# A gated delta-rule block on one core: the two lowest of four inverse-merge levels on narrow tiles, and the state evictions moved to ScalarE

## The reference, cut to what matters

```python
def step(S, inp):
    qt, kt, vt, gt, bt = inp
    S = S * jnp.exp(gt)[..., None, None]
    mem = jnp.einsum('bhk,bhkv->bhv', kt, S)
    delta = (vt - mem) * bt[..., None]
    S = S + jnp.einsum('bhk,bhv->bhkv', kt, delta)
    o = jnp.einsum('bhk,bhkv->bhv', qt * scale, S)
    return (S, o)
```

## Time and profile before

| | |
|---|---|
| median of 3 runs | 2520.83 us (2520.28 to 2522.46) |
| the profiled execution's own time | 2518.24 us |
| its span, first to last instruction | 2516.3 us |
| mean granted TensorE clock | 0.978 |
| PE busy | 2352.5 us, 93% |
| DVE busy | 2004.9 us, 80% |
| ACT busy | 1407.4 us, 56% |
| POOL busy | 1279.2 us, 51% |

### The profile page before, as it was taken

One profiled execution on the slowest core, in us unless ns is written; L12 is line 12 of the kernel. 1 busy time (PEld: TensorE's weight loads), 2 busy tenths in 40 slices (PEclk: granted clock), 3 DMA queues, 4 the chain that ended last, 5 costly groups with the idle time before them and its releaser, 6 DMA issues. The chain is left out here.

```text
span 2516.3 us, 53535 instructions
## 1 busy us (share of the span) xinstructions
PE 2352.5 (93%) x18800; PEld 1889.7 (75%) x18800; DVE 2004.9 (80%) x4146; ACT 1407.4 (56%) x3331; POOL 1279.2 (51%) x2046
## 2 busy tenths in 40 slices
PE   6599999999999999999999999999999998699997
PEld 2378888888888888888888888888888887546665
DVE  5678888888888888888888888888888887235544
ACT  3256666666666666666666666666666665322221
POOL 3456566666666666666666666656566665100000
PEclk9689999999999999999999999999999999799998
DMA  4211121112111211121112111211121110221100
GB/s 129 69 36 35 27 61 34 34 33 55 35 36 36 54 37 35 36 54 36 36 36 55 36 36 36 55 36 36 36 55 36 36 26 9 66 62 34 34 9 9
DMA packets 203849, 103.20 MB, mean 41 GB/s; under 512 B 97009, under 2 KB 185018, under 8 KB 203586
## 3 DMA queue, kind: packets, MB, share of 16 engines
q1 hardware_dynamic: 203266, 99.65, 17.0%
q10 hardware_dynamic: 320, 0.13, 0.0%
HBM read 69.89 MB, written 2.54 MB: 29 GB/s over the span
## 5 line engine op out<-in xcount | busy, mean ns | idle before, releaser
L861 DVE SCALAR_TENSOR_TENSOR dr_y<-dr_ps,cw,dr_y 128x255 f32<-128x255 f32 (+2 forms) x1152 | 479.9, 472 | 8.9 <-ACT dr_y L986 8.9
L1125 POOL TENSOR_TENSOR dr_fo<-dr_vo,dr_nhalf 128x4 f32<-128x4 f32 x128 | 156.1, 1219 | 539.5 <-DVE dr_vo L941 539.5
L744 PE MATMUL dr_ps<-dr_w,dr_am 128*128 128x96 f32 x3072 | 418.1, 280 | 3.2 <-ACT dr_w L1038 3.2
L744 PEld LDWEIGHTS dr_ps<-dr_w,dr_am 128*128 128x128 f32 x3072 | 380.3, 193 | 12.1 <-ACT dr_w L1038 3.9
L831 DVE TENSOR_TENSOR dr_w<-dr_ps,mask 128x512 bf16<-128x512 f32 x512 | 350.3, 684 | 31.4 <-PE dr_ps L629 24.6
L986 ACT ACTIVATE dr_y<-dr_ps,cw 128x256 f32<-128x256 f32 x384 | 160.9, 470 | 195.1 <-PE dr_ps L676 195.0
L1038 ACT COPY dr_w<-dr_ps 128x384 f32<-128x384 f32 x384 | 188.8, 492 | 134.8 <-PE dr_ps L744 134.8
L972 ACT CAST dr_tn<-dr_ps 128x512 bf16<-128x512 f32 x384 | 226.3, 589 | 55.7 <-PE dr_ps L644 55.6
L873 DVE TENSOR_TENSOR_SCAN dr_dec<-dr_abc,dr_dg 128x512 f32<-128x512 f32 x128 | 208.4, 1628 | 33.4 <-POOL dr_dg L1091 18.1
L975 ACT CAST dr_tt<-dr_ps 128x512 bf16<-128x512 f32 x384 | 233.5, 608 | 0.0
L650 PE MATMUL dr_ps<-dr_tt,dr_w 128*128 128x128 bf16 x2048 | 197.9, 219 | 20.1 <-DVE dr_w L831 20.1
(11 more groups left out here) (204 smaller groups left out, 5059.9 us busy)
## 6 DMA issues: line engine op xcount, KB each, us to landing
dr_abc<-scr_a SPq DMA_DIRECT2D x64, 512.0 KB, 5.4
dr_qk<-dr_sy SPq DMA_DIRECT2D x384, 48.0 KB, 2.0
dr_bcb<-scr_b SPq DMA_DIRECT2D x128, 64.0 KB, 4.6
dr_c<-dr_b SPq DMA_DIRECT2D x512, 4.0 KB, 1.8
dr_qk<-dr_sy SPq DMA_DIRECT2D x128, 32.0 KB, 1.9
ex_modb<-scr_mod SPq DMA_DIRECT2D x4, 1024.0 KB, 8.1
wv<-in_Wv SPq DMA_DIRECT2D x8, 384.0 KB, 3.5
wo<-in_Wo SPq DMA_DIRECT2D x1, 3072.0 KB, 12.1
```

The source lines that it names most:

```text
L744: last = pe.matmul(ps[:, bank, h * DV:(h + 1) * DV], wt(h), x[:, h * DV:(h + 1) * DV], start=(start and h == 0), stop=(h == QH - 1), skip_ ...
L861: v.scalar_tensor_tensor(y[:, slot, x:T], ps[:, BANK[n], off:off + T - x], cw[:, t, TAPS - 1 - x:TAPS - x], y[:, slot, x:T], ALU.mult, ALU ...
```

## The change

The two lowest levels (8 to 16, 16 to 32) no longer work on 128x128 tiles. What is not zero there fits in 32 columns per unit. A new POOL piece `block` makes `b32`, the part of `b16` inside the 32x32 diagonal blocks. `narrow1` is a matmul of `b32` with `c32t` (32 columns, all 8 units in one bank) and one masking eviction to `w32` by DVE; `narrow2` is one matmul with `tt`, evicted by ACT to `c32t`; `widen` (DVE) transposes `c32t` to `c32` and expands it to the new `tt`, and after the second narrow level `tn` too. The two upper levels stay as they were. The eviction of `S` moves from DVE to ACT, in front of the squares of the same piece. `PLAN` is another table.

```diff
-LEVELS = 4
-LVL0 = 3
+NARROW = 2
+LEVELS = 2
+LVL0 = 5
...
             def merge1(st, l, g):
                 it, m = st
                 if l == 0:
-                    pe.wait_ge(s["te_ok"], it * 2 + 1)
-                    if g == 0:
-                        pe.wait_ge(s["ab_ok"], it + 1)
-                        wait(pe, s["tt_ok"], (it * LEVELS - 1) * 2 + 1 if it else 0)
+                    pe.wait_ge(s["te_ok"], it * (NARROW + 2) + NARROW + 1)
...
+            def narrow1(st, l):
+                it, m = st
+                if l == 0:
+                    pe.wait_ge(s["ab_ok"], it + 1)
+                    pe.wait_ge(s["b32_ok"], (it + 1) * CH)
+                    pe.wait_ge(s["c32t_ok"], it * (NARROW + 1) + 1)
+                else:
+                    pe.wait_ge(s["cn_ok"], it * NARROW + l)
+                for u in range(U):
+                    last = pe.matmul(ps[:, X0, u * 4 * BASE:(u + 1) * 4 * BASE], b32[:, u, :], c32t[:, u, :],
+                                     start=True, stop=True)
+                last.then_inc(s["n1_ps"], 1)
+
+            def narrow2(st, l):
+                it, m = st
+                pe.wait_ge(s["wn_ok"], it * NARROW + l + 1)
+                pe.wait_ge(s["te_ok"], it * (NARROW + 2) + l + 1)
+                if l == 0:
+                    wait(pe, s["tt_ok"], it * LEVELS * 2)
+                for u in range(U):
+                    last = pe.matmul(ps[:, X1, u * 4 * BASE:(u + 1) * 4 * BASE], tt[:, u, :], w32[:, u, :],
+                                     start=True, stop=True)
+                last.then_inc(s["n2_ps"], 1)
...
             def expand(st):
                 it, m = st
                 v.wait_ge(s["xb_ok"], it + 1)
+                wait(v, s["te_ok"], it * (NARROW + 2))
...
                 v.wait_ge(s["c32_ok"], it + 1)
-                v.transpose(c32t[:].rearrange("p u i -> p (u i)"), c32[:].rearrange("p u i -> p (u i)")
-                            ).then_inc(s["c32t_ok"], 1)
+                turned(c32t, c32).then_inc(s["c32t_ok"], 1)
                 wait(v, s["p3"], it * LEVELS * 2)
...
+                spread(tt, c32).then_inc(s["te_ok"], 1)
+
+            def narrow1(st, l):
+                it, m = st
+                v.wait_ge(s["n1_ps"], it * NARROW + l + 1)
+                wait(v, s["n2_ps"], it * NARROW + l)
+                v.tensor_tensor(w32[:], ps[:, X0, 0:NCOL].rearrange("p (u n) -> p u n", u=U), bc(maskn[:, l, :], 1, U),
+                                ALU.mult).then_inc(s["wn_ok"], 1)
+
+            def widen(st, l):
+                it, m = st
+                v.wait_ge(s["cn_ok"], it * NARROW + l + 1)
+                v.wait_ge(s["te_ok"], it * (NARROW + 2) + l + 1)
+                if l == NARROW - 1:
+                    spread(tn, c32t).then_inc(s["te_ok"], 1)
+                turned(c32, c32t).then_inc(s["c32t_ok"], 1)
+                v.wait_ge(s["c32t_ok"], it * (NARROW + 1) + l + 2)
+                spread(tt, c32).then_inc(s["te_ok"], 1)
...
+            def narrow2(st, l):
+                it, m = st
+                act.wait_ge(s["n2_ps"], it * NARROW + l + 1)
+                act.wait_ge(s["c32t_ok"], it * (NARROW + 1) + l + 1)
+                act.copy(c32t[:], ps[:, X1, 0:NCOL].rearrange("p (u n) -> p u n", u=U)).then_inc(s["cn_ok"], 1)
...
+            def state(st):
+                it, m = st
+                act.wait_ge(s["s_ps"], it + 1)
+                for side in range(2):
+                    lo = 64 * side
+                    act.copy(S[lo:lo + 64, :, side * DV:(side + 1) * DV],
+                             ps[lo:lo + 64, CX, 0:QV].rearrange("p (a n) -> p a n", a=PAIRS)[:, :, side * DV:(side + 1) * DV]
+                             ).then_inc(s["S_ok"], 1)
+                squares(st, 0)
...
+            def block(st):
+                it, m = st
+                wait(pool, s["n1_ps"], it * NARROW)
+                for c in range(CH):
+                    us = slice(c * QH, (c + 1) * QH)
+                    pool.wait_ge(s["b16_ok"], it * CH + c + 1)
+                    pool.tensor_tensor(b32[:, us, :], b16[:, m, us, :], bc(bd32[:], 1, QH), ALU.mult).then_inc(s["b32_ok"], 1)
```

`spread(dst, src)` is the multiply with `bd32` that `expand` held, and `turned(dst, src)` the transpose. Of the new table two lines:

```diff
+        (23.53, ("block",)), (24.9, ("rows",)), (25.89, ("base",)), (29.53, ("expand",)), (30.44, ("narrow1", 0)),
+        (30.64, ("narrow2", 0)), (30.75, ("widen", 0)), (31.96, ("narrow1", 1)), (33.43, ("narrow2", 1)),
```

More of the change, by code:

```diff
@@ L61 @@
 ATANH = [1.0 / (2 * k + 1) for k in range(9)]
[L63 to L70, removed]
[5 rows of a table removed]
[L76 to L80, removed]
@@ L539, in slots @@
                     on[piece[0]](stages[k], *piece[1:])
+        NCOL = U * 4 * BASE
+        wide = lambda ap: ap.rearrange("p u (n i) -> p u n i", i=4 * BASE)
         def run(eng, on):
@@ L547, in delta_rule @@
         PIECES = ("merge1", "merge2", "w0", "delta", "residual", "ks", "out", "state_out", "mean", "gated", "oT", "wo",
-                  "acc", "rows", "base", "expand", "proj", "silu", "taps", "gate", "norms", "gains", "root", "keys_gain", "decays", "keys", "keys_scale", "scores", "decayed", "negate",
+                  "acc", "rows", "block", "base", "expand", "narrow1", "narrow2", "widen", "proj", "silu", "taps", "gate", "norms", "gains", "root", "keys_gain", "decays", "keys", "keys_scale", "scores", "decayed", "negate",
                   "values", "round")
@@ L812, in wo_ @@
                 last.then_inc(s["wo_ps"], 1)
-            on.update(merge1=merge1, merge2=merge2, rows=rows_, proj=proj, norms=norms, gate=gate, keys=keys, scores=scores,
+            on.update(merge1=merge1, merge2=merge2, rows=rows_, narrow1=narrow1, narrow2=narrow2, proj=proj, norms=norms, gate=gate, keys=keys, scores=scores,
                       values=values, w0=w0, residual=residual, delta=delta, out=outputs, state_out=state_out, ks=ks,
@@ L953, in acc @@
                 v.tensor_tensor(at, at, ps[:, CO, 0:D], ALU.add).then_inc(s["acc_ok"], 1)
-            on.update(merge1=merge1, expand=expand, taps=taps, decays=decays, gains=gains, decayed=decayed, values=values,
-                      residual=residual, state_out=state, ks=ks, mean=mean, gated=gated, acc=acc)
+            on.update(merge1=merge1, expand=expand, narrow1=narrow1, widen=widen, taps=taps, decays=decays, gains=gains, decayed=decayed, values=values,
+                      residual=residual, ks=ks, mean=mean, gated=gated, acc=acc)
             v.reciprocal(beta, beta).then_inc(s["bq_ok"], 1)
@@ L1065, in turn_out @@
                                    scale=gw[:, t:t + 1]).then_inc(s["oT_ok"], 1)
-            on.update(merge2=merge2, rows=rows_, proj=proj, silu=silu, gate=gate, keys=keys, negate=negate, round=round_,
-                      w0=w0, delta=delta, state_out=lambda st: squares(st, 0), out=squares, ks=ks, oT=turn_out)
+            on.update(merge2=merge2, rows=rows_, narrow2=narrow2, proj=proj, silu=silu, gate=gate, keys=keys, negate=negate, round=round_,
+                      w0=w0, delta=delta, state_out=state, out=squares, ks=ks, oT=turn_out)
             act.wait_ge(s["c_ld"], 32)
+            act.wait_ge(s["set_ok"], 5)
             run(act, on)
@@ L1144, in base @@
                     ins.then_inc(s["xb_ok"] if j == BASE - 2 else s["xs"], 1)
-            on.update(keys_scale=keys_scale, base=base, silu=squares, gains=gains, root=root, keys_gain=keys_gain, negate=select, mean=scale)
+            on.update(keys_scale=keys_scale, base=base, block=block, silu=squares, gains=gains, root=root, keys_gain=keys_gain, negate=select, mean=scale)
             pool.memset(qk[:], 0.0).then_inc(s["set_ok"], 1)
@@ L1605, in constants @@
     c[:, C_IOTA:C_IOTA + E] = np.arange(E)
+    for l in range(NARROW):
+        size, col = BASE << l, i // (4 * BASE) * (4 * BASE)
+        at = col[:, None] + np.arange(4 * BASE)
+        same = i[:, None] // (2 * size) == at // (2 * size)
+        other = i[:, None] // size != at // size
+        c[:, C_NARROW + l * 4 * BASE:C_NARROW + (l + 1) * 4 * BASE] = (same & other) | (i[:, None] == at)
     c[:, C_HALF:C_HALF + 2] = (i[:, None] // BASE) % 2 == np.arange(2)
```

44 lines of the change are left out of this document (27 added, 17 removed), and 8 rows, old and new, of the table PLAN.

## The result

The changed kernel took 2453.11 us (median of 4 runs, 2447.86 to 2458.4) against 2520.93 us of the kernel before on the same chip: a ratio of 0.973 with a 95% interval of 0.9702 to 0.9758. It is 68 us faster; 48 had been forecast. The profiled execution is the slowest of the four, 2458.4 us with a span of 2456.4 us; 2518.24 and 2516.3 us had been the pair before. So the two profiled executions are 60 us apart, and the traces explain these 60. The other 8 us between the medians lie in the spread of the changed kernel's runs: two are at 2448 us with a mean granted clock of 0.979 and 0.980, two at 2458 us with 0.973 and 0.975. A difference to the changed kernel's median is therefore sure to some 5 us only, or 0.1 us a turn.

What follows compares the result with a forecast made beforehand. PE's queue sets the pace, its waits being for DVE. Per turn 1.52 us less PE work, minus 1.45 new waits, plus 0.6 old ones gone, gives 0.67, taken as 0.75; times 64, 48 us: 2473 us, range 2420 to 2522.

Steps and rivals of the forecast that it cites:

- The narrow matmul: PE's queue: each 32-column matmul takes 35 ns, 32 a turn add 1.12 us against 2.64 us removed.
- DVE's work: DVE per turn: expansions and narrow masks added, wide masks and `S` copies removed, net +0.53 us, 28.8 us in all.
- ACT and POOL: Both have idle room for their changed work; only ACT's order counts, with `ks` waiting 0.1 us behind the `S` copies.
- Second `residual`: Second chunk on PE: waits 0.55 us because ACT's `w` eviction stands behind that of the second projection.
- Second `narrow2`: PE waits 0.45 us for its DVE mask, which stands behind the first `widen` and `gated`.
- First `narrow1`: PE waits 0.15 us for `c32t`, since `expand` cannot start before POOL's chain ends.
- The first wide `merge2`: PE waits 0.2 us for a mask behind the 2.55 us of the second `widen` on DVE.
- The two old waits: PE's waits before the first merge and at the mask behind the `values` transposes go, 0.3 us each.
- doubled count: The walk counts a wait twice when one shift serves two, so 0.67 us a turn was raised to 0.75.
- B: Rival, chance 0.20: PE's time turns into waits over DVE; turn 31.7 to 31.9 us, 2500 to 2526 us.
- A: Rival, chance 0.18: PE's whole gain of 1.52 us a turn comes through; turn 30.3 us, 2424 us.
- C: Rival, chance 0.16: POOL's `gs` falls under DVE's expansion, costing up to 1.04 us a turn; 2540 us at full price.

Runs made afterwards that it cites:

- two runs: Eviction of `S` alone moved to ACT in the kernel before: 2520.5 us; moved back to DVE in the changed kernel: 2454.1 us.
- third of three edits: First `gated` put behind the second narrow mask on DVE, against the changed kernel with the `w`-wait reorder and early `xb` copy: 2390.37 us, from 2407.77.
- fastest version: Changed kernel with second chunk's first residual and delta moved earlier, `xb` copy ahead of `block`, and first `gated` behind the second narrow mask: 2390.37 us.

## Why the prediction was right, step by step

**The bound.** That PE's queue set the pace, with waits for DVE, is shown: 78% of added PE work came through before. That waits between the engines take over after the change is shown by the 29%.

**The narrow matmul was priced too high.** 0.035 us forecast, 0.025 measured. The 0.035 us came from the listed time of 14 loads, 0.56 us, which is not what they occupy the queue for. In the changed kernel the loads are listed with 0.56 us too, but the 14 matmuls of `rows`, with nothing to wait for ahead of the next, take 0.41 us from start to start, 29 ns each:

```profile
1394.47 0.57 PE L666 MATMUL dr_ps<-dr_c,sel 128*128 128x64 bf16 x14
1394.88 0.41 PE L744 MATMUL dr_ps<-const,dr_qk 128*128 128x128 f32 x2
```

With 25 ns the net of PE is 2.64 - 0.80 = 1.84 us, not 1.52, and PE's busy time fell by 1.91. The Trainium skill (TensorE: Matmul & The Clock Gate, Back-to-back issue gap) gives about 25 ns for an isolated matmul of 1 to 64 columns. This trace shows that gap at 32 columns even with fresh weights for each matmul, and 29 ns at 64. The 81 ns that the Trainium skill gives there for a pair of load and matmul at 128 columns isn't what this trace shows (56 ns, before and after).

**DVE's work was priced too high.** Forecast +0.53 us, measured -0.61. The expansion was taken at 1.04 to 1.11 us; it takes 0.69 in the median of 192. Four expansions at some 0.4 us less make 1.6 us; `c32`, 0.83 us where 0.45 was taken, gives 0.4 back. What the rows of before held was a wait for POOL, see below. That DVE would be no longer well behind PE was therefore wrong: it is idle for 3.33 us a turn, 2.3 forecast. That each chain over it counts was right: one expansion more costs nothing where DVE waits anyway, and a mask moved ahead of `gated` is worth 17 us.

**ACT and POOL.** Mostly as forecast. The gate in front covers the moved eviction: the copies of `S` end at 1404.27 us and `ks` starts at 1404.32, without the 0.1 us of wait that was forecast. The eviction itself was worth nothing either way (two runs).

**The new waits.** The walk along the queues had them in the right places. Second `residual`: forecast 0.55, measured 0.56 us of idle, and worth 28 us when removed (0.44 us a turn). Second `narrow2`: 0.45 with its start against 0.34 us of idle, worth 17 us as the third of three edits. First `narrow1`: 0.15 against 0.37, because `c32` took 0.83 us; worth 17 us. The first wide `merge2`: 0.2 forecast, none found, since the second `widen` is 0.8 us shorter than priced. Not forecast: 0.58 us ahead of the first chunk's `delta`, whose residual stands on DVE behind the third taps and the gains, and the gains take 0.40 us longer than before, under POOL's `gs`. Sum 1.85 us, forecast 1.45; at the three places that were named it is 1.27 us, forecast 1.15. The two old waits that were to go went, and so did the third that the prediction had read, 0.34 us ahead of the scores, which its sum left in place: PE's old idle fell by 0.78 us, forecast 0.6.

**The sum.** 0.75 us a turn forecast, 0.84 measured in the turn and 0.90 on average. PE's net work was taken 0.39 us too small (1.52 against 1.91) and the new waits 0.40 us too small (1.45 against 1.85), which cancels; the old waits make the rest: 1.91 - 1.85 + 0.78 = 0.84. So the agreement to 0.1 us is in good part luck. The step from 0.67 to 0.75 us had no row behind it, and no run shows the doubled count that it stands for. A turn of 30.8 us, the lower end of the forecast, would be 2455 us and not 2445, and B's turns of 31.7 to 31.9 us are 2513 to 2526; the measured turn and time lie inside either reading of the forecast.

**The rivals.** A, the whole gain, is not what happened, but is nearly reached by reordering (turn 29.91 us in the fastest version, where A had 30.3, and 29.9 with the measured gain). B, PE's time turned into waits, is what the changed kernel does under the old table, but there the waits cost more than PE gains: 2588 us lies above anything that B or C gave. C's mechanism is there: `gs` is held up by the expansion, by 0.46 us and not 1.04, and `gated` waits 0.72 us for it where it had waited 1.28; it is the same wait that the third edit moved off the mask. It didn't make the kernel slower than before, and under the old table it isn't there: `gs` takes its 0.83 us, and only a select ahead of it is longer (1.10 us). That neither half of the change gains anything without the other was no rival and should have been one.

## What to carry to other kernels

A cheaper operation in a hand-ordered pipeline is worth only what the order lets through: here the same tiles were 68 us slower or 68 us faster by the table alone. Laying the new queues beside each other, with durations from the trace, found three of the four places where PE then idled, and three small edits to them gave another 63 us. Before a duration is carried over from a trace, it is to be compared with the minimum and the median of all instructions of its shape, and with what the other engine ran at that moment: a long one may hold a wait. The minimum of one line can mislead: `tn` was never under 0.95 us before the change, but its twin `tt`, the same shape one line on, had a minimum of 0.68 us.
